# Graph attention on one core: 0-or-1 matrices made in the step that uses them, four slots of row records, and edge attributes encoded by two matmuls of 512 columns a block

## What is computed

```python
h = (x @ W.T).reshape(n, H, D)
h_src, h_dst = h[src], h[dst]
alpha = einsum('ehd,hd->eh', h_src, a_src) + einsum('ehd,hd->eh', h_dst, a_dst)
enc = relu(edge_attr @ edge_W.T + edge_b).reshape(-1, H, D)
alpha = alpha + sum(enc * h_dst, axis=-1)
alpha = where(alpha >= 0, alpha, 0.2 * alpha)
amax = segment_max(alpha, dst, num_segments=n)
ex = exp(alpha - amax[dst])
denom = segment_sum(ex, dst, num_segments=n)
attn = ex / maximum(denom[dst], 1e-10)
out = segment_sum(h_src * attn[..., None], dst, num_segments=n)
return out.reshape(n, H * D) + bias
```

## Time and profile before

| | |
|---|---|
| median of 3 runs | 3568.86 us (3564.5 to 3572.67) |
| profiled execution | 3549.46 us, its span 3547.7 us |
| PE, busy share of the span | 68% |
| DVE | 64% |
| POOL | 54% |
| ACT | 28% |
| edge loop, first to last start of the scores' first instruction | 213.4 to 2967.6 us, 110 steps, so 25.3 us from one to the next |

### The profile page before, as it was taken

The page is one execution under the profiler, slowest core; times in us unless marked ns, Lnnn a source line. Parts: engine busy times, 40 slices in busy tenths (PEclk is TensorE's granted clock), DMA queues, the critical chain, the costliest instruction groups (busy, mean ns, idle before and its releaser), DMA issues. The chain is left out here.

```text
span 3547.7 us, 36332 instructions
## 1 busy us (share of the span) xinstructions
PE 2421.1 (68%) x8642; PEld 1634.9 (46%) x8642; DVE 2273.3 (64%) x3546; ACT 986.2 (28%) x2822; POOL 1904.2 (54%) x2041
## 2 busy tenths in 40 slices
PE   1647667776667667676677767777676554269998
PEld 1424444444444444444444444444444333168887
DVE  7957767776667677776667777776666554251223
ACT  3522222222222222222222222222222221043332
POOL 3656656666666566666666656666666442607000
PEclk9857777777778677877777777777777676559999
DMA  8355555556555555556555555556556883300000
GB/s 270 124 136 153 154 147 153 150 149 178 147 154 154 144 155 145 159 149 177 151 152 154 150 150 155 147 156 174 150 154 134 124 121 53 88 27 3 21 18 31
DMA packets 341609, 471.12 MB, mean 133 GB/s; under 512 B 115596, under 2 KB 262718, under 8 KB 341170
## 3 DMA queue, kind: packets, MB, share of 16 engines
q0 software_dynamic: 90000, 262.14, 30.0%
q1 hardware_dynamic: 250578, 206.73, 20.0%
q10 hardware_dynamic: 848, 0.26, 0.0%
HBM read 380.17 MB, written 88.72 MB: 132 GB/s over the span
## 5 line engine op out<-in xcount | busy, mean ns | idle before, releaser
L1003 POOL DMA_INDIRECT src_in<-t_node_rows,rec_in x1760 | 1681.5, 955 | 1112.4 <-issue 552.2
L1065 PE MATMUL p_sum<-weighted,hot 128*128 128x264 f32 x3520 | 1262.5, 520 | 610.5 <-issue 420.9
L1065 PEld LDWEIGHTS p_sum<-weighted,hot 128*128 128x128 f32 x3520 | 875.2, 259 | 975.6 <-issue 703.7
L1210 DVE SCALAR_TENSOR_TENSOR prod<-p_enc,near 128x512 f32<-128x512 f32 x880 | 563.1, 680 | 421.7 <-ACT near L1132 355.8
L1260 DVE TENSOR_TENSOR weighted<-src_in,p_turn 128x1024 f32<-128x1024 f32 x440 | 534.5, 1215 | 326.6 <-remote 129.8
L1214 DVE TENSOR_REDUCE dots<-prod 128x32 f32<-128x1024 f32 x440 | 536.9, 1220 | 15.2
L1043 PE MATMUL p_pick<-win,hotT 128*128 128x272 f32 x880 | 383.2, 523 | 192.5 <-ACT near L1132 88.3
L1112 ACT ACTIVATE hot<-apart 128x128 f32<-128x128 f32 x440 | 136.2, 309 | 1336.5 <-issue 543.8
L1132 ACT COPY near<-p_pick 128x272 f32<-128x272 f32 x440 | 169.4, 385 | 680.4 <-remote 391.3
L1036 PE MATMUL p_enc<-expander,attrT 30*128 30x256 bf16 x1760 | 314.7, 305 | 43.2 <-DMA attrT<-t_block_attr 42.9
L1043 PEld LDWEIGHTS p_pick<-win,hotT 128*128 128x128 f32 x880 | 154.2, 220 | 301.7 <-issue 200.9
(11 more groups left out here) (334 smaller groups left out, 1623.5 us busy)
## 6 DMA issues: line engine op xcount, KB each, us to landing
win<-t_node_rows SPq DMA_DIRECT2D x440, 136.0 KB
t_block_sums<-sums SPq DMA_DIRECT2D x110, 528.0 KB
places<-t_block_places SPq DMA_DIRECT2D x110, 256.0 KB
src_in<-t_node_rows,rec_in POOLq DMA_INDIRECT x1760
attrT<-t_block_attr SPq DMA_DIRECT2D x330, 36.0 KB
t_node_rows<-out_rows SPq DMA_DIRECT2D x49, 136.0 KB, 1.7
x<-in_x SPq DMA_DIRECT2D x4, 1536.0 KB, 25.6
out_x<-x SPq DMA_DIRECT2D x48, 128.0 KB
```

The source lines that it names most:

```text
L1003: pool.indirect_dma_start(src[:, q.par, b, k, :], None, scr["rows"], bass.IndirectOffsetOnAxis(ap=rec_i[:, q.par, b, k:k + 1], axis=0)).th ...
L1065: last = nc.tensor.matmul(p_sum[b % 2][:, 0:ROW], hot[:, q.par, b, :], weighted[:, b, k, :], start=(k == 0), stop=(k == W - 1))
L1210: nc.vector.scalar_tensor_tensor(prod[:, 2 * half:2 * half + 2, :], p_enc[(PAIRS * b + half) % len(p_enc)][:, :, :], 0.0, near[:, q.par, b ...
```

## The change

Three parts.

1. `hot` of step q's blocks is made in step q itself, where it was made a step ahead: on ACT, hot(q,0) stands behind near(n,1), hot(q,1) behind near(n,2), hot(q,2) behind the exponentials, hot(q,3) behind near(n,3) and ahead of `hotT`. The row records, which it reads, have four slots (ROWS_RING), and `load_rows` waits for gathers and `hot` of the step four before. At the start of the loop, only `near` is made.
2. The attributes lie in DRAM as 36 rows of 128 a block (row of attribute and slot), the encoder's matrix is block-diagonal, 111 x 1024, and PE encodes a block by two matmuls of 512 columns with 111 rows. The attribute loads take 36 rows of 1 KB each for 9 of 4 KB, the stores go in four DMAs of 256-byte pieces for one of 1024-byte pieces, and DVE reads and writes the attributes in another order when it parts them.
3. The encoder's matrix takes 24 small DMAs of POOL for 6 and a memset; `enc_left` shares memory with `ro`, with a wait on DVE for it; the memset of `attrT` is 111 x 1024 for 30 x 4096.

```diff
-KE = 3 * (KA + 1)
+KE = 3 * (W * KA + 1)
+STORES = 3 + W
...
-    nc.sync.dma_start(scr["block_attr"].rearrange("c (b s) -> b c s", s=SLOTS)[block, :, :], parts[0:n, :, :]).then_inc(stored, 16)
+    table = scr["block_attr"].rearrange("(k c) (b r) -> k b c r", k=W, r=P)
+    for k in range(W):
+        nc.sync.dma_start(table[k, block, :, :], parts[0:n, :, k * P:(k + 1) * P]).then_inc(stored, 16)
...
-    of = parts[:, EF * i:EF * (i + 1), :]
+    of = parts[:, EF * i:EF * (i + 1), :].rearrange("p f (k r) -> p f k r", k=W)
+    attrs = attrs.rearrange("p f (r k) -> p f k r", k=W)
...
+            nc.gpsimd.memset(keep["expander"][:, :], 0.0).then_inc(s["enc_zero"], 1)
...
             for j in range(3):
-                pool.dma_start(keep["expander"][KA * j:KA * (j + 1), :], enc_p[0:KA, j, :]).then_inc(s["enc_moved"], 16)
-                pool.dma_start(keep["expander"][3 * KA + j:3 * KA + j + 1, :], enc_p[KA:KA + 1, j, :]).then_inc(s["enc_moved"], 16)
+                for k in range(W):
+                    row = KA * (W * j + k)
+                    pool.dma_start(keep["expander"][row:row + KA, k * D:(k + 1) * D], enc_p[0:KA, j, :]).then_inc(s["enc_moved"], 16)
+                    row = KA * W * 3 + j
+                    pool.dma_start(keep["expander"][row:row + 1, k * D:(k + 1) * D], enc_p[KA:KA + 1, j, :]).then_inc(s["enc_moved"], 16)
...
+            dve.wait_ge(s["enc_split"], 4)
...
+ROWS_RING = 4
...
             def load_rows(q):
-                if q.since(RING):
-                    before = q.prev().prev()
+                if q.s >= ROWS_RING:
+                    before = straight(q.s - ROWS_RING)
                     for b in range(Q):
-                        sp.wait_ge(s_src[q.par][b], 16 * W * q.turn)
+                        sp.wait_ge(s_src[before.par][b], 16 * W * (before.turn + 1))
                     sp.wait_ge(s["hot"], Q * (before.s + 1))
...
-                    for j in range(2):
-                        k = 2 * half + j
-                        slots = attrT[:, q.par, b, :].rearrange("c (r k) -> c k r", k=W)[:, k, :]
-                        last = nc.tensor.matmul(p_enc[(PAIRS * b + half) % len(p_enc)][:, j, :], slots, keep["expander"][:, :], start=True, stop=True)
-                    last.then_inc(s["enc"], 1)
+                    nc.tensor.matmul(p_enc[(PAIRS * b + half) % len(p_enc)][:, :, :].rearrange("p j d -> p (j d)"), attrT[:, q.par, b, :],
+                                     keep["expander"][:, 2 * half * D:(2 * half + 2) * D], start=True, stop=True).then_inc(s["enc"], 1)
...
             def body(q, ahead=2):
                 n, before = q.next(), q.prev()
-                if ahead:
-                    make_hot(n, 1)
                 if q.since(1):
                     move_sums(before, 1)
                 if ahead:
                     move_near(n, 1)
-                    make_hot(n, 2)
+                make_hot(q, 0)
                 if q.since(1):
                     move_sums(before, 2)
                 keep_tops(q)
                 if ahead:
                     move_near(n, 2)
-                    make_hot(n, 3)
+                make_hot(q, 1)
                 weights(q)
+                make_hot(q, 2)
                 if q.since(1):
                     move_sums(before, 3)
                 if ahead:
                     move_near(n, 3)
+                make_hot(q, 3)
                 if ahead > 1:
                     make_hotT(n.next())
-                    make_hot(n.next(), 0)
                 move_sums(q, 0)
                 if ahead > 1:
                     move_near(n.next(), 0)
...
-            for b in range(Q):
-                front(straight(0), b)
-            front(straight(1), 0)
+            for b in range(Q):
+                move_near(straight(0), b)
+            move_near(straight(1), 0)
```

More of the change, by code:

```diff
@@ L260, in prologue @@
         enc_f = m.sb("enc_f", [KA + 1, D])
-        enc_left = m.sb("enc_left", [KA + 1, D])
+        enc_left = ro[0:KA + 1, :, :].rearrange("p r w -> p (r w)")[:, 0:D]
         enc_p = m.sb("enc_p", [KA + 1, 3, D], BF16)
@@ L291, in prologue @@
             attrs_out based moved attr_made rows_out table_stored base_made base_stored base_loaded
-            dummy_made dummy_stored bias_loaded merge_consts""".split()
+            dummy_made dummy_stored bias_loaded merge_consts enc_zero""".split()
         s = {n: m.sem("s_" + n) for n in names}
@@ L378, in _ @@
             sp.wait_ge(s["base_loaded"], 16)
-            sp.wait_ge(s["table_stored"], 64)
+            sp.wait_ge(s["table_stored"], 16 * STORES)
             sp.wait_ge(s["dummy_stored"], 32)
@@ L459, in _ @@
                     nc.gpsimd.tensor_tensor(at(x_all, i * 5 + u), at(x_all, i * 5 + u), bias[:, :], ALU.add)
-            pool.wait_ge(s["enc_moved"], 96)
+            pool.wait_ge(s["enc_moved"], 96 * W)
             pool.wait_ge(s["merge_consts"], 9)
@@ L801, in edge_loop @@
     with Scope(nc) as m:
-        rec = m.sb("rec_in", [P, RING, Q, W + 1])
+        rec = m.sb("rec_in", [P, ROWS_RING, Q, W + 1])
         rec_i = rec[:, :, :, :].bitcast(I32)
-        attrT = m.sb("attrT", [KE, RING, Q, SLOTS], BF16)
+        attrT = m.sb("attrT", [KE, RING, Q, P], BF16)
         flags = m.sb("flags_in", [Q * H, RING, P + 1])
@@ L848, in edge_loop @@
         row_of = lambda v: v.rearrange("p (q h) -> p q h", q=Q)
-        s_rec = [m.sem(f"s_rec_loaded{i}") for i in range(RING)]
+        s_rec = [m.sem(f"s_rec_loaded{i}") for i in range(ROWS_RING)]
         s_attr = [m.sem(f"s_attr_loaded{i}") for i in range(RING)]
@@ L895, in load_attr @@
                     sp.wait_ge(s["enc"], PAIRS * Q * (q.prev().s))
-                cols = scr["block_attr"].rearrange("c (n e) -> n c e", e=Q * SLOTS)
+                cols = scr["block_attr"].rearrange("c (n e) -> n c e", e=Q * P)
                 v = block_of(cols, q.s)
                 for j in range(3):
-                    sp.dma_start(attrT[KA * j:KA * (j + 1), q.par, :, :].rearrange("c q e -> c (q e)"), v).then_inc(s_attr[q.par], 16)
+                    sp.dma_start(attrT[W * KA * j:W * KA * (j + 1), q.par, :, :].rearrange("c q e -> c (q e)"), v).then_inc(s_attr[q.par], 16)
             def load_flags(q):
@@ L976, in _ @@
                     if u == LOADED_AT:
-                        sp.wait_ge(s["table_stored"], 64 * (i + 1))
+                        sp.wait_ge(s["table_stored"], 16 * STORES * (i + 1))
                     body(straight(RING + i * turn + u))
@@ L991, in gather @@
             def gather(q):
-                pool.wait_ge(s_rec[q.par], 16 * (q.turn + 1))
+                pool.wait_ge(s_rec[q.s % ROWS_RING], 16 * (q.s // ROWS_RING + 1))
                 nc.gpsimd.sem_inc(s["waited_by_pool"], 1)
@@ L1104, in make_hot @@
                 if b == 0:
-                    act.wait_ge(s_rec[q.par], 16 * (q.turn + 1))
+                    act.wait_ge(s_rec[q.s % ROWS_RING], 16 * (q.s // ROWS_RING + 1))
                 if b or q.since(1):
                     act.wait_ge(s["hot"], n)
-                nc.scalar.activation(apart[:, :], keep["node_at"][:, :], ACT.Abs, bias=rec[:, q.par, b, W:W + 1]).then_inc(s["apart"], 1)
+                nc.scalar.activation(apart[:, :], keep["node_at"][:, :], ACT.Abs, bias=rec[:, q.s % ROWS_RING, b, W:W + 1]).then_inc(s["apart"], 1)
                 act.wait_ge(s["apart"], n + 1)
@@ L1345, in expand @@
                     if i:
-                        dve.wait_ge(s["table_stored"], 64 * i)
+                        dve.wait_ge(s["table_stored"], 16 * STORES * i)
                     make_rows_of(nc, x, words, group(keep["base"]), group(keep["base_mod"]), small, ro, head_flags, item[:, i + 1, 1:2], group(last_ok))
@@ L1980, in edge_part @@
         keep = dict(
-            whole, node_at=m.sb("node_at", [P, P]), expander=m.sb("expander", [KE, D], BF16),
+            whole, node_at=m.sb("node_at", [P, P]), expander=m.sb("expander", [KE, W * D], BF16),
             base_i=m.sb("base_i", [1, BLOCKS], I32), tops=m.sb("block_tops", [Q * H, STEPS, 2]),
```

10 lines of the change are left out of this document (4 added, 6 removed).

## The result

| | before | with the change |
|---|---|---|
| median, 12 runs each, one chip | 3569.19 us | 3589.13 us (3578.54 to 3600.48) |
| ratio | | 1.0053, 95% interval 1.0034 to 1.0072 |
| profiled span | 3547.7 us | 3583.5 us |
| first gather starts | 183.5 us | 191.0 us |
| scores of the first to the last step | 213.4 to 2967.6 us, 2754.2 us | 220.45 to 3003.56 us, 2783.1 us |

Slower by 0.53%, where 0.3% faster was forecast. Of the 36 us between the two profiled executions 7 lie ahead of the loop and 29 in it. The medians lie 20 us apart.

What follows compares the result with a forecast made beforehand. Bound: a ring of POOL's gathers, pick, `near`, and scores, exponentials, `weighted`, `p_sum`. Terms -14 - 4 + 8 - 3 + 3 = -10 us on the profiled 3549.5 gave 3539.5, as a median 3559 us; range 3480 to 3622.

Steps and rivals of the forecast that it cites:

- The casts with strided operands ... 0: DVE's parting of attributes, 0.96 us a cast: 0 us; some +2 in the prologue were each twice as long.
- The opening: What bounds the loop: POOL busiest, 16 gathers making 20 us of a 25.3 us step, then waiting 407.9 us for `near`.
- ACT's order, -14 - 4 + 8: `hot` no longer delays exponentials (-14 us) or `sums` and `near` (-4); later `apart` and `hot` delay block 0's pick (+8).
- PE's encoding, 0: Two matmuls for four a block, same 1024 columns streamed: 0 us, with a bound of -107 us for fewer weight loads.
- rival of fewer instructions: 14% fewer PE matmuls shorten the remote waits on PE alike: -73 us, 3486 us; chance 0.19.
- SP, 0: SP's row loads no longer wait for gathers (165.2 us in 38 waits); what they feed rarely waited: 0 us.
- loads meet the gathers: Rival: SP's earlier loads disturb landing gathers, doubling DVE's 72.1 us of waits: +72 us, 3631 us; chance 0.09.
- Small pieces: Prologue's attribute store in 4608 pieces of 256 bytes: +3 us; as a rival +18 instead, 3574 us, chance 0.06.
- Memset, -3: Prologue's memset of `attrT`, 3.47 us for 4096 values a partition, now 1024: -3 us.
- POOL's DMAs, 0: 18 further DMAs of POOL, 9.6 us, fit a hole of 10.21 us: 0, at most +1 us.
- The burst: Rival: ACT's work after a late word of PE grows, delaying block 3's `near` and block 0's pick: +45, 3614 us; chance 0.19.
- The signs: Wrong if `near`'s remote waits move over 50 us, POOL's idle over 20, `raw`'s waits double, or block 3's `near` follows `hot` unwaited.

Runs made afterwards that it cites:

- slow conditions: Groups of runs, not tied to a chip's number, in which the unedited kernel before took 3534 us (first, fourth) or 3568 us (last).
- fast conditions: Second and third groups of runs, not tied to a chip's number, in which the unedited kernel before took 3065 us.
- the gate: load_rows waits again for the gathers of two steps before, as in the kernel before; put into the changed kernel alone: 1.0065 of the kernel before.
- the first group: Four edits against the kernel before (3534 us): ACT's order with four slots 0.9988, encoding alone 1.0051, changed kernel with contiguous casts 0.9959, four slots alone 0.9992.

## Why the prediction was wrong

- **"The casts with strided operands ... 0".** This is the step that failed. It allowed 2 us in the prologue "were each twice as long", put nothing for the loop at all and nothing for the subtractions, and so kept a bound that was far too small. The casts are three times as long (2.85 for 0.95 us, the subtraction 2.87 for 1.76), 7.9 us in the prologue and 24 in the loop. The two runs of slow conditions that differ in nothing else lie 15 to 21 us apart, more than the forecast's whole gain of 10 us; two of fast conditions lie 67 to 73 us apart for 72 us of casts. The rows were there: the trace of the kernel before had 20 casts and subtractions of 1536 values, 15 of them in the loop. The opening calls POOL the busiest of the engines that work in every step; by the table it is busy for 54% and DVE for 64%, and none of DVE's own work in the loop is weighed.
- **ACT's order, -14 - 4 + 8.** Alone it gave 0.9988 with an interval of 0.2% to both sides, which holds the forecast's -10 us (0.9972) and nothing. In fast conditions with the gate it is 0.9997. The term of -14 took 65 waits of `weighted` to become shorter by 0.21 us each; with the order alone they were 84, and 213 us for 197, so no gain is seen there, though `hot` left the chain as foreseen. The cost was there too: the wait ahead of block 0's pick grew, its median from 0.887 to 1.875 us:

```profile
L1055 PEldq EVENT_SEMAPHORE  x110: 51/1875/6253, 198.7 to 2966.2; - x110
```

  That is 0.99 us a step, where 0.63 in a quarter of the steps was taken. With the order alone it was 2.374 us, and the time did not grow. Why it costs nothing isn't shown.
- **PE's encoding, 0.** Nothing speaks against it: four matmuls or two made no difference in fast conditions. The rival of fewer instructions was about the remote waits of slow conditions, and falls there: those of `near` and `weighted` were 521 us and are 531, with 120 us moved from the one to the other, and the encoding with contiguous casts and the gate gained nothing (1.0005).
- **SP, 0, and the rival "loads meet the gathers".** Right in slow conditions (0.9992), wrong as a statement on the kernel: in fast conditions the same edit costs 3.4%. The rival's price was 72 us for doubled waits of `raw`; measured were 98 us more of these waits (1.5 times, not twice) and 103 us in the median.
- **Small pieces.** The +3 came as +1.3, and not by the sum that gave it: that set 45 ns for each new piece against the 8.3 us from issue to landing, where the old 1152 pieces at 45 ns take 3.2 us. The pieces did move more slowly: while they ran the DMA engines moved 216 GB/s (171 to 176 us), for 345 GB/s before (161.5 to 164.5). The Trainium skill ("DMA: Bandwidth & Descriptors", Specifications) has 512 bytes as the least for full rate, and the trace agrees in direction. But four issues took 3.28 us of SP for 0.37, so issuing and moving overlapped, and how the 1.3 us divide between them isn't shown. The rival's +18 is far off.

```profile
161.50:164.50 3.00, 0.00 (x0) 0.00 (x0) 2.83 (x5) 0.00 (x0) 0.00 (x0) 0.50 1.01 345
```
```profile
171.00:176.00 5.00, 0.00 (x0) 0.00 (x0) 4.76 (x8) 0.00 (x0) 0.00 (x0) 0.50 0.87 216
```

  The first is the kernel before, the second the changed one; the last two numbers are the DMA engines' busy share and the GB/s.
- **Memset, -3.** Right: 2.56 us. **POOL's DMAs, 0.** Right, since the first gather of the loop waits for the rows, not for POOL.
- **The burst.** `near` of block 3 behind `hot`: no cost is seen in the run of ACT's order alone.
- **The signs.** Two of those listed as "wrong" came: the remote waits of `near` fell by 120 us, and POOL's idle time rose by 50 us, from 1112.4 to 1162.0. They told that something was off, not what: with the casts contiguous and the gate the first was still there (292.8 us), at 1.0005.

## What to carry to other kernels

A view with other strides is a change of cost, not of form: price it for each engine instruction that uses it, and count these over the whole program, the loop's side work too. Here between half and all of it landed on the path, by the conditions. A wait that throttles transfers may be doing good: before taking it away, ask what it keeps apart, and test where the loop runs at the transfers' pace. A list of waits shows where waiting ended up, not what made the time longer. The engines' busy times, before and after, pointed at DVE (28.6 us more), but at ACT as well (33 us more, which the run of ACT's order alone has too, at no loss): it takes the lines that changed their mean time, and an edit that puts them back.

## What was not expected of the hardware

- DVE: 1536 f32 values a partition to bf16 took 0.95 us side by side, 2.85 us when the reads jump by 16 bytes, and 6.97 us when the writes jump by 256 bytes. The Trainium skill ("VectorE: DVE Perf Modes", What auto-detection actually checks) lets a copy of one source keep its fast mode where the outermost dimensions of both sides are even or equal, as they are here (3 and 3). The conditions of that mode ask nothing of the inner step. By them alone one would have forecast 0.95 us for the strided cast too, and the trace has 2.85; whether it ran in another mode isn't shown. The subtraction has two sources and slowed as well, from 1.76 to 2.87 us. ACT took 2.93 us for its strided copy of as many.
- The kernel before took 3534 to 3569 us in three groups and in the result, and 3065 us in two. In the latter the remote waits of `near` (391 us in the earlier trace rows) are gone, and the granted clock is higher (0.826 for 0.763 in the profiled executions), which may be cause or consequence. What makes PE's results reach the others late in the slow conditions stays open; no edit here removed these waits.
- The granted clock rose with the encoding (0.763 to 0.795 in the profiled executions; 0.762 and 0.798 in the first group), both between the levels of 1.2 and 2.4 GHz, and the time did not follow. PE's busy time fell by 193 us, and the kernel was not faster for it.
